# Silu of the gate in the feed-forward and expert steps: ScalarE's own function in place of tanh and a VectorE operation

## The chip, the cores and the metric

The kernel runs on one core of one Trainium2 chip. The metric is the device time of one execution in microseconds (us), as the median of several runs. Beside it stands one profiled execution, from which all durations below are read. TensorE (PE) does the matrix products, VectorE (DVE) and GpSimd (POOL) the elementwise work, ScalarE (ACT) the functions, and SyncE issues the transfers.

## What is computed

Four sequences of 512 positions and width 512 pass through two decoder layers, each of three residual blocks with a layer norm behind each. What matters here are the state scans and the two gated steps:

```python
def _L0_ffn_ref(x, w_gate, w_up, w_down):            # 512 -> 2048 -> 512
    gated = jax.nn.silu(gate) * up
...
def _swiglu(x, wg, wu, wd):                          # 8 experts of 352 and a shared one of 1408
    return jax.nn.silu(x @ wg) * (x @ wu) @ wd
...
def step(state, inp):                                # scan over time, 16 states per channel
    d, b, c, u = inp
    dA = jnp.exp(d[..., None] * A)
    state = state * dA + (d * u)[..., None] * b[:, None, :]
    y = jnp.einsum('bdn,bn->bd', state, c)
```

All eight experts are computed for each position, and their hidden values are multiplied by the routing weight. silu(x) is x times the logistic function of x, which is also x (1 + tanh(x/2)) / 2.

## The kernel before

Everything is held with the channel on the 128 partitions and the 512 positions of one sequence along the free dimension. The four sequences are computed one after the other, three in a loop and the last behind it. The dense products run in bfloat16 in three parts (high by high, high by low, low by high: `product`, L262 to L266), so one 128 by 128 block of weights costs three matmuls of 512 columns.

The gated steps are in `hidden_and_scan`. It runs once per sequence as "ffn" (16 tiles of 128 hidden channels) beside the state scan of the following block (16 blocks of 32 channels), and once as "moe" (33 tiles: 22 of the experts, 11 of the shared one) beside the first scan of the next sequence (32 blocks). The last sequence's "moe" has no scan beside it. Before the first sequence it runs once with a scan and no tiles. So there are 4 feed-forward stages of 16 tiles and 4 expert stages of 33, 196 tiles in all.

In each stage a loop over steps is written out for each engine, and this writing alone sets the order. In a step:

- **TensorE** spreads the scan's u dt and dt over the states for the blocks to come (`spread_dtx`, L673, and `spread_dt`, L661: fp32 matmuls on 32 rows), then `gate` and `up` of the next tile (12 matmuls each), every fourth step `reduce_quad` (L682, the sum over states), then one `down_piece` (up to 12 matmuls), whose bank is free again when VectorE has taken the piece before it (`taken`). `spread_dt(s)` waits until `decays(s - 1)` has read the one bank of dt.
- **ScalarE** does `decays` (L754: four exps of 128 by 511 from PSUM, into one of two buffers `da`, so it waits for the scan of two blocks earlier) and then `gate_tanh` (L761), which reads the gate bank and writes tanh(x/2) into one of two buffers `t2`. Both are in program order: the tanh of tile j stands between the exps of blocks j and j + 1. It waits for the gate product and, from tile 2 on, for `hid` of two tiles earlier.
- **VectorE** does `scan` (L794), `inputs` of the next block (L785), `take_down` (L831, L834), every fourth step `finish_y` (L799), then `silu_gate` (L804), `times_up` (L812), in the expert stages `times_weight` (L820, one to three pieces by partition), `low_part` (L248) and, in the expert stages every fourth step, `inputs_of` (L789). In the expert stages TensorE's `spread_dtx` needs the result of `inputs_of`.
- **GpSimd** multiplies each scanned block by the output rows (L869); `reduce_quad` waits for four of these.

silu thus takes three operations: tanh(x/2) on ScalarE, (t + 1) x on VectorE, and times_up with the factor 0.5. `silu`, the semaphore that VectorE raises, also tells TensorE that a gate bank is free (`gate` of tile j waits for tile j - 2).

```python
    def gate_tanh(jt):
        act.wait_ge(gate_mm, jt + 1)
        if jt >= 2:
            act.wait_ge(hid, jt - 1)
        act.activation(t2[jt % 2], gate_bank(jt), ACT.Tanh, scale=0.5).then_inc(th, 1)
...
    def silu_gate(jt):
        dve.wait_ge(th, jt + 1)
        dve.scalar_tensor_tensor(out=t2[jt % 2], in0=t2[jt % 2], scalar=1.0, in1=gate_bank(jt),
                                 op0=ALU.add, op1=ALU.mult).then_inc(silu, 1)
```

ScalarE's functions lie in sets of tables. The compiler puts an ACT_TABLE_LOAD before an operation whose function isn't in the set that is active. exp and tanh share a set, so the gated stages had no load inside.

Of the kernel before, what the change touches and what calls it, by code (L numbers as in the profile page):

```python
# [8 lines left out]
ALU = mybir.AluOpType  # L9
ACT = mybir.ActivationFunctionType  # L10
# [39 lines left out]
def chunk_of(tiles, j):  # L50

    return (j - first_chunk(tiles)) // CHUNK + 1
# [193 lines left out]
def low(engine, out, x):  # L246

    return engine.tensor_tensor(out, x, high(x), ALU.subtract)  # L248
# [338 lines left out]
def hidden_and_scan(nc, k, tag, tiles, slot, which, gated, last, splitter=None):  # L587
# [14 lines left out]
    with ExitStack() as ctx:  # L602
        def sem(name):
            return k.sem(f"{tag}_{name}")
# [3 lines left out]
        def split_now(step, lag=0):  # L608

            if not splitter or step >= blocks:  # L610
                return []
            count = len(splitter.slots)
            first, end = [at * (count + 2) // blocks for at in (step, step + 1)]
            return [n - lag for n in range(first, end) if 0 <= n - lag < count]
        gate_mm, up_mm, th, silu, hid, weighted = [sem(n) for n in ("gate_mm", "up_mm", "th", "silu", "hid", "weighted")]
        hidlo, xsplit, down, taken = [sem(n) for n in ("hidlo", "xsplit", "down", "taken")]
        dt_mm, dtx_mm, decay = [sem(n) for n in ("dt_mm", "dtx_mm", "decay")]
        dtx_in = sem("dtx_in")
# [2 lines left out]
        t2 = k.moe_t if gated else k.ffn_t  # L621
        xlo = k.moe_xlo if gated else k.ffn_xlo
        held, held_lo = k.held, k.held_lo
        HELD = 2 * CHUNK
# [5 lines left out]
        def down_bank(p):  # L630
            return k.ps[:, 3 + p % KM if last_chunk(p) else 7, :]

        def gate_bank(jt):
            return k.ps[:, 3 + jt % 2, :]

        def up_bank(jt):
            return k.ps[:, 5 + jt % 2, :]

        def states(s):
            return k.states[s % NB]  # L640

        def quartet(s):
            return states(s).rearrange("p (n t) -> p n t", n=GRP)

        def weight_pieces(jt):
            return expert_pieces(jt) if jt < ROUTED else [(0, P, NEXP)]

        @blk.sync
        def _(sp):
            stream_block(k, sp, slot + (hidden_slots(tiles) if tiles else 0), last)  # L650
            if splitter:
                splitter.move(sp)
# [94 lines left out]
        @blk.scalar  # L747
        def _(act):
            def decays(s):
                act.wait_ge(dt_mm, s + 1)  # L750
                if s >= 2:
                    act.wait_ge(scanned, s - 1)
                for n in range(GRP):
                    a = act.activation(k.da[s % 2][:, n, 1:T], dt_bank[:, 1:T], ACT.Exp, scale=rate[:, GRP * s + n:GRP * s + n + 1])  # L754
                a.then_inc(decay, 1)

            def gate_tanh(jt):
                act.wait_ge(gate_mm, jt + 1)
                if jt >= 2:
                    act.wait_ge(hid, jt - 1)  # L760
                act.activation(t2[jt % 2], gate_bank(jt), ACT.Tanh, scale=0.5).then_inc(th, 1)  # L761

            if blocks:
                decays(0)
            if tiles:
                gate_tanh(0)
            for step in range(steps):
                if step + 1 < blocks:
                    decays(step + 1)
                if step + 1 < tiles:  # L770
                    gate_tanh(step + 1)
                for n, late in zip_longest(split_now(step), split_now(step, 2)):
                    if late is not None and splitter.by_pe(late):
                        splitter.take_rest(act, late)
                    if n is not None:
                        splitter.high_part(act, n)

        @blk.vector
        def _(dve):

            def inputs(s):
                dve.wait_ge(dtx_mm, s + 1)
                if s >= NB:
                    dve.wait_ge(reduced, (s - NB) // 4 + 1)
                dve.tensor_tensor(quartet(s), dtx_bank[:, None, :].broadcast_to([P, GRP, T]), k.in_rows, ALU.mult).then_inc(inp, 1)  # L785

            def inputs_of(j):

                dve.tensor_tensor(k.dtx_now[:, j % 2, :], dt[:, j, :], y[:, j, :], ALU.mult).then_inc(dtx_in, 1)  # L789

            def scan(s):
                dve.wait_ge(decay, s + 1)
                dve.wait_ge(inp, s + 1)
                dve.tensor_tensor_scan(states(s), k.da[s % 2][:, :, :].rearrange("p n t -> p (n t)"), states(s), 0.0,  # L794
                                       ALU.mult, ALU.add).then_inc(scanned, 1)

            def finish_y(j):
                dve.wait_ge(reduced, j + 1)
                dve.scalar_tensor_tensor(out=y[:, j, :], in0=y[:, j, :], scalar=skip[:, j:j + 1], in1=y_bank,  # L799
                                         op0=ALU.mult, op1=ALU.add).then_inc(yout, 1)  # L800

            def silu_gate(jt):
                dve.wait_ge(th, jt + 1)
                dve.scalar_tensor_tensor(out=t2[jt % 2], in0=t2[jt % 2], scalar=1.0, in1=gate_bank(jt),  # L804
                                         op0=ALU.add, op1=ALU.mult).then_inc(silu, 1)

            def times_up(jt):
                dve.wait_ge(silu, jt + 1)
                dve.wait_ge(up_mm, jt + 1)
                if jt >= HELD:  # L810
                    dve.wait_ge(down, KM * chunk_of(tiles, jt - HELD) + KM)
                dve.scalar_tensor_tensor(out=held[:, jt % HELD, :], in0=t2[jt % 2], scalar=0.5, in1=up_bank(jt),  # L812
                                         op0=ALU.mult, op1=ALU.mult).then_inc(hid, 1)

            def times_weight(jt):

                h = held[:, jt % HELD, :]
                dve.wait_ge(hid, jt + 1)
                for a, b, e in weight_pieces(jt):
                    op = dve.tensor_tensor(h[a:b, :], h[a:b, :], k.gates[a:b, e, :], ALU.mult)  # L820
                op.then_inc(weighted, 1)

            def low_part(jt):
                dve.wait_ge(weighted if gated else hid, jt + 1)
                low(dve, held_lo[jt % HELD], held[:, jt % HELD, :]).then_inc(hidlo, 1)

            def take_down(p):
                m = p % KM
                dve.wait_ge(down, p + 1)
                if p < KM:  # L830
                    dve.tensor_copy(k.xc[:, m, :], down_bank(p)).then_inc(taken, 1)  # L831
                else:
                    dve.wait_ge(taken, p + 1 - KM)
                    dve.tensor_tensor(k.xc[:, m, :], k.xc[:, m, :], down_bank(p), ALU.add).then_inc(taken, 1)  # L834

            if which == 0:
                inputs_of(0)
            if tiles:
                for c in range(KM):
                    low(dve, xlo[:, c, :], k.xr[:, c, :]).then_inc(xsplit, 1)  # L840
            if blocks:
                inputs(0)
            for step in range(steps):
                if step < blocks:
                    scan(step)
                    for n in split_now(step, 1):
                        if not splitter.by_pe(n):
                            splitter.low_part(dve, n)
                if step + 1 < blocks:
                    inputs(step + 1)  # L850
                if LAG <= step < pieces + LAG:
                    take_down(step - LAG)
                if step % 4 == 1 and 5 <= step <= blocks + 1:
                    finish_y(step // 4 - 1)
                if step < tiles:
                    silu_gate(step)
                    times_up(step)
                if gated and step < tiles:
                    times_weight(step)
                if step < tiles:  # L860
                    low_part(step)
                if which == 0 and step % 4 == 2 and step + 2 < blocks:
                    inputs_of(step // 4 + 1)
# [1035 lines left out]
```

## Time and profile before

| | us |
|---|---|
| median of 3 runs | 4571.92 (4571.24 to 4577.19) |
| profiled execution, its own time | 4570.23 |
| its span, first to last instruction | 4568.5 |
| TensorE busy (matmul) | 3618.0, 79% |
| VectorE busy | 3404.5, 75% |
| ScalarE busy | 1331.6, 29% |
| GpSimd busy | 1275.6, 28% |
| mean granted TensorE clock | 0.87 |

The profile's page shows two engines near three quarters busy. It doesn't say which of them ends a wait in a given stage, so the stages are read one by one from the timelines, whose rows give the start, the duration, the engine, the line and what released the engine after an idle time. A matmul's duration there is longer than its spacing, since matmuls overlap. The stages repeat: the sixteen tanh operations of the four feed-forward stages span 145.69, 145.67, 145.70 and 145.69 us from first to last, the thirty-three of the three expert stages with a scan 334.51, 334.48 and 334.48.

### The profile page before, as it was taken

To read this page: it belongs to the slowest core of one execution; us is meant where nothing else is said; L and a number is where in the kernel's file an instruction comes from. 1 tells how busy PE (TensorE), PEld (TensorE's weight loads), DVE (VectorE), ACT (ScalarE), POOL (GpSimd) and SP (SyncE) were. 2 spreads that over 40 slices of the span, in tenths; PEclk is the share of its full clock that TensorE was granted. 3 is DMA by queue.
4 is the path that set the end of the run, shared out by engine and by line. 5 is a ranking of instruction groups with operands and counts; after the bars stand their busy time and mean duration, and the time that the engine had idled before them with its cause. 6 is when DMAs were issued, how large, how long until landed. Compare 5 with 4: busy or idle time off the path is not lost. (4 is left out here: it accounts for less than half of the span.)

```text
span 4568.5 us, 40958 instructions
## 1 busy us (share of the span) xinstructions
PE 3618.0 (79%) x15151; PEld 1519.7 (33%) x15151; DVE 3404.5 (75%) x3068; ACT 1331.6 (29%) x2010; POOL 1275.6 (28%) x440
## 2 busy tenths in 40 slices
PE   5777769846999769857899778965899976984798
PEld 2222333313333333313433333322433323331443
DVE  5989479575899569785799757876699847967444
ACT  4666332114322233113322233211422233211201
POOL 1544114321344104331244202332144311432000
PEclk8888879867999879878799988977799987986899
DMA  4888212201222202111122211110122121220122
GB/s 150 307 325 305 102 35 76 69 14 44 70 76 76 90 27 76 63 35 53 54 76 70 95 42 62 63 56 30 49 76 70 67 97 34 78 69 15 62 97 79
DMA packets 69035, 380.85 MB, mean 83 GB/s; under 512 B 7648, under 2 KB 7776, under 8 KB 66784
## 3 DMA queue, kind: packets, MB, share of 16 engines
q1 hardware_dynamic: 68832, 378.15, 23.7%
q8 instruction: 127, 2.08, 0.2%
q14 instruction: 76, 0.62, 0.0%
HBM read 314.16 MB, written 63.96 MB: 83 GB/s over the span
## 5 line engine op out<-in xcount | busy, mean ns | idle before, releaser
L265 PE MATMUL ps<-r,ring 128*128 128x512 bf16 (+1 forms) x1912 | 751.9, 394 | 0.0
L262 PE MATMUL ps<-xr,ring 128*128 128x512 bf16 x1696 | 681.3, 402 | 33.2 <-DVE r L248 19.9
L266 PE MATMUL ps<-xr,ring 128*128 128x512 bf16 x1696 | 678.7, 400 | 0.0
L869 POOL TENSOR_TENSOR hh<-hh,bc 128x2048 f32<-128x2048 f32 x72 | 336.3, 4671 | 1020.7 <-DVE hh L794 1020.7
L262 PE MATMUL ps<-r,ring 128*128 128x512 bf16 (+4 forms) x1160 | 464.6, 401 | 102.8 <-DVE xc L834 38.3
L754 ACT ACTIVATE da<-ps,params_sb 128x511 f32<-128x511 f32 x768 | 463.1, 691 | 83.5 <-PE ps L661 57.6
L266 PE MATMUL ps<-r,ring 128*128 128x512 bf16 (+4 forms) x1160 | 464.5, 401 | 0.0
L869 POOL TENSOR_TENSOR bc<-bc 128x2048 f32<-128x2048 f32 x64 | 301.1, 4705 | 390.2 <-DVE bc L794 390.2
L869 POOL TENSOR_TENSOR r<-r,bc 128x2048 f32<-128x2048 f32 x56 | 261.9, 4677 | 322.7 <-DVE r L794 322.7
L794 DVE TENSOR_TENSOR_SCAN hh<-da,hh 128x2048 f32<-128x2048 f32 x72 | 326.0, 4527 | 1.5
L794 DVE TENSOR_TENSOR_SCAN bc<-da,bc 128x2048 f32<-128x2048 f32 x64 | 291.6, 4556 | 0.5
L262 PEld LDWEIGHTS ps<-xr,ring 128*128 128x128 bf16 x1696 | 168.0, 99 | 371.9 <-issue 187.3
L661 PE MATMUL ps<-r,squares_sb 32*128 32x512 f32 x384 | 234.0, 691 | 58.5 <-PEq L1710 31.4
L761 ACT ACTIVATE row<-ps 128x512 f32<-128x512 f32 x100 | 59.7, 597 | 744.4 <-PE ps L266 744.4
L262 PE MATMUL ps<-bc,ring 128*128 128x512 bf16 (+3 forms) x416 | 175.0, 421 | 123.3 <-DMA ring<-wsplit 39.2
L834 DVE TENSOR_TENSOR xc<-xc,ps 128x512 f32<-128x512 f32 x176 | 119.6, 680 | 199.3 <-PE ps L266 199.3
L265 PEld LDWEIGHTS ps<-r,ring 128*128 128x128 bf16 (+1 forms) x1912 | 189.0, 99 | 236.4 <-issue 30.9
L794 DVE TENSOR_TENSOR_SCAN r<-da,r 128x2048 f32<-128x2048 f32 x56 | 254.4, 4542 | 0.6
L266 PEld LDWEIGHTS ps<-xr,ring 128*128 128x128 bf16 x1696 | 166.8, 98 | 235.0 <-issue 28.8
L761 ACT ACTIVATE r<-ps 128x512 f32<-128x512 f32 x96 | 57.3, 597 | 603.8 <-PE ps L266 603.8
L262 PEld LDWEIGHTS ps<-r,ring 128*128 128x128 bf16 (+4 forms) x1160 | 113.1, 98 | 330.2 <-issue 174.5
L201 PE MATMUL ps<-r,squares_sb 128*128 128x512 f32 x282 | 175.5, 709 | 52.3 <-ACT ring L226 20.3
(232 smaller groups left out, 6655.0 us busy)
## 6 DMA issues: line engine op xcount, KB each, us to landing
ring<-wsplit SPq DMA_DIRECT2D x304, 768.0 KB, 4.2
r<-wstream SPq DMA_DIRECT2D x76, 768.0 KB, 7.5
wsplit<-ring SPq DMA_DIRECT2D x58, 768.0 KB, 4.8
wsplit<-r SPq DMA_DIRECT2D x18, 768.0 KB, 5.9
bc<-xT SPq DMA_DIRECT2D x4, 1024.0 KB, 5.6
xr<-xT SPq DMA_DIRECT2D x4, 1024.0 KB, 9.4
bc<-guwT SPq DMA_DIRECT2D x4, 1024.0 KB, 11.2
out<-xr SPq DMA_DIRECT2D x4, 1024.0 KB, 3.9
```

The source lines that it names most:

```text
L201: pe.matmul(self.banks[:, c, :], ident, self.whole[n % SPLIT_RING][:, at], start=True, stop=False)
L262: mm = pe.matmul(out, w_hi, x_hi, start=start, stop=False)
L265: pe.matmul(out, w_hi, x_lo, start=False, stop=False)
L266: return pe.matmul(out, w_lo, x_hi, start=False, stop=stop)
L661: pe.matmul(dt_bank, k.headmean[at, :], dt[at, s // 4, :], start=True, stop=True).then_inc(dt_mm, 1)
L754: a = act.activation(k.da[s % 2][:, n, 1:T], dt_bank[:, 1:T], ACT.Exp, scale=rate[:, GRP * s + n:GRP * s + n + 1])
L761: act.activation(t2[jt % 2], gate_bank(jt), ACT.Tanh, scale=0.5).then_inc(th, 1)
L794: dve.tensor_tensor_scan(states(s), k.da[s % 2][:, :, :].rearrange("p n t -> p (n t)"), states(s), 0.0, ALU.mult, ALU.add).then_inc(scanne ...
L834: dve.tensor_tensor(k.xc[:, m, :], k.xc[:, m, :], down_bank(p), ALU.add).then_inc(taken, 1)
L869: pool.tensor_tensor(quartet(s), quartet(s), k.out_rows, ALU.mult).then_inc(read, 1)
```

## The change

ScalarE computes silu directly from the gate bank. `silu_gate` goes away, `times_up` becomes a plain product, and `silu` is raised by ScalarE.

```diff
--- before.py
+++ after.py
@@ -612,7 +612,7 @@
             count = len(splitter.slots)
             first, end = [at * (count + 2) // blocks for at in (step, step + 1)]
             return [n - lag for n in range(first, end) if 0 <= n - lag < count]
-        gate_mm, up_mm, th, silu, hid, weighted = [sem(n) for n in ("gate_mm", "up_mm", "th", "silu", "hid", "weighted")]
+        gate_mm, up_mm, silu, hid, weighted = [sem(n) for n in ("gate_mm", "up_mm", "silu", "hid", "weighted")]
         hidlo, xsplit, down, taken = [sem(n) for n in ("hidlo", "xsplit", "down", "taken")]
         dt_mm, dtx_mm, decay = [sem(n) for n in ("dt_mm", "dtx_mm", "decay")]
         dtx_in = sem("dtx_in")
@@ -754,21 +754,21 @@
                     a = act.activation(k.da[s % 2][:, n, 1:T], dt_bank[:, 1:T], ACT.Exp, scale=rate[:, GRP * s + n:GRP * s + n + 1])
                 a.then_inc(decay, 1)
 
-            def gate_tanh(jt):
+            def gate_silu(jt):
                 act.wait_ge(gate_mm, jt + 1)
                 if jt >= 2:
                     act.wait_ge(hid, jt - 1)
-                act.activation(t2[jt % 2], gate_bank(jt), ACT.Tanh, scale=0.5).then_inc(th, 1)
+                act.activation(t2[jt % 2], gate_bank(jt), ACT.Silu).then_inc(silu, 1)
 
             if blocks:
                 decays(0)
             if tiles:
-                gate_tanh(0)
+                gate_silu(0)
             for step in range(steps):
                 if step + 1 < blocks:
                     decays(step + 1)
                 if step + 1 < tiles:
-                    gate_tanh(step + 1)
+                    gate_silu(step + 1)
                 for n, late in zip_longest(split_now(step), split_now(step, 2)):
                     if late is not None and splitter.by_pe(late):
                         splitter.take_rest(act, late)
@@ -799,18 +799,12 @@
                 dve.scalar_tensor_tensor(out=y[:, j, :], in0=y[:, j, :], scalar=skip[:, j:j + 1], in1=y_bank,
                                          op0=ALU.mult, op1=ALU.add).then_inc(yout, 1)
 
-            def silu_gate(jt):
-                dve.wait_ge(th, jt + 1)
-                dve.scalar_tensor_tensor(out=t2[jt % 2], in0=t2[jt % 2], scalar=1.0, in1=gate_bank(jt),
-                                         op0=ALU.add, op1=ALU.mult).then_inc(silu, 1)
-
             def times_up(jt):
                 dve.wait_ge(silu, jt + 1)
                 dve.wait_ge(up_mm, jt + 1)
                 if jt >= HELD:
                     dve.wait_ge(down, KM * chunk_of(tiles, jt - HELD) + KM)
-                dve.scalar_tensor_tensor(out=held[:, jt % HELD, :], in0=t2[jt % 2], scalar=0.5, in1=up_bank(jt),
-                                         op0=ALU.mult, op1=ALU.mult).then_inc(hid, 1)
+                dve.tensor_tensor(held[:, jt % HELD, :], t2[jt % 2], up_bank(jt), ALU.mult).then_inc(hid, 1)
 
             def times_weight(jt):
 
@@ -853,7 +847,6 @@
                 if step % 4 == 1 and 5 <= step <= blocks + 1:
                     finish_y(step // 4 - 1)
                 if step < tiles:
-                    silu_gate(step)
                     times_up(step)
                 if gated and step < tiles:
                     times_weight(step)
```

The lines of the new kernel behind L799 stand 7 lower than those of the old (`times_up` is L807).

On ScalarE, in the feed-forward stage from tile 2 on, the order before was this (two steps; `da` are the exps of `decays`, `row` and `r` the two buffers `t2`; a wait is shown by the first name that its semaphore had in the program, so `first_landed2` and `first_stored2` are `hid` and `gate_mm` here, `prep0_gdone` and `prep0_weights_in` are `scanned` and `dt_mm`):

```order
L754 ACTIVATE da<-ps,params_sb 128x511 [waits prep0_gdone,prep0_weights_in]
L754 ACTIVATE da<-ps,params_sb 128x511 x3
L761 ACTIVATE row<-ps 128x512 [waits first_landed2,first_stored2]
L754 ACTIVATE da<-ps,params_sb 128x511 [waits prep0_gdone,prep0_weights_in]
L754 ACTIVATE da<-ps,params_sb 128x511 x3
L761 ACTIVATE r<-ps 128x512 [waits first_landed2,first_stored2]
```

Now there are two table loads in each step. Of the two waits the load carries the one for the buffer (`prep0_gsplit` is `scanned`, `first_landed3` is `hid`), the function behind it the one for its input (`prep0_spread` is `dt_mm`, `first_stored2` is `gate_mm`):

```order
L754 ACT_TABLE_LOAD [waits prep0_gsplit]
L754 ACTIVATE da<-ps,params_sb 128x511 [waits prep0_spread]
L754 ACTIVATE da<-ps,params_sb 128x511 x3
L761 ACT_TABLE_LOAD [waits first_landed3]
L761 ACTIVATE row<-ps 128x512 [waits first_stored2]
L754 ACT_TABLE_LOAD [waits prep0_gsplit]
L754 ACTIVATE da<-ps,params_sb 128x511 [waits prep0_spread]
L754 ACTIVATE da<-ps,params_sb 128x511 x3
L761 ACT_TABLE_LOAD [waits first_landed3]
L761 ACTIVATE r<-ps 128x512 [waits first_stored2]
```

So a load can run before its function's input is there. Counted over the whole program this gives 126 loads more as written (31 in a feed-forward stage, 63 in an expert stage with a scan, 1 in the last one), and with the loop 4 x 31 + 3 x 63 + 1 = 314 in an execution.

On VectorE, one step of the feed-forward stage before (L794 is the scan; this listing names it by its operand form):

```order
L794 SCALAR_TENSOR_TENSOR bc<-da,bc 128x2048
L785 TENSOR_TENSOR bc<-ps,bc 128x2048
L804 SCALAR_TENSOR_TENSOR row<-row,ps 128x512
L812 SCALAR_TENSOR_TENSOR r<-row,ps 128x512
L248 TENSOR_TENSOR ctxTs<-r 128x512
L794 SCALAR_TENSOR_TENSOR bc<-da,bc 128x2048
```

and now:

```order
L794 SCALAR_TENSOR_TENSOR bc<-da,bc 128x2048
L785 TENSOR_TENSOR bc<-ps,bc 128x2048
L807 TENSOR_TENSOR r<-row,ps 128x512
L248 TENSOR_TENSOR ctxTs<-r 128x512
L794 SCALAR_TENSOR_TENSOR bc<-da,bc 128x2048
```

One operation of 128 by 512 leaves each step, and the product by `up` is a TENSOR_TENSOR. Nothing else moves on any engine.

## Rows read from the trace of the kernel before

**Rows 1.** Windows: from:to, us; busy PE, PEld, DVE, ACT, POOL; clock, DMA share, GB/s

```profile
638.00:822.00 184.00, 176.38 (x768) 66.23 (x768) 159.90 (x104) 46.91 (x80) 73.31 (x16) 0.94 0.23 78
1147.00:1520.00 373.00, 348.83 (x1594) 134.04 (x1594) 352.73 (x268) 96.58 (x165) 146.98 (x32) 0.98 0.22 72
4270.00:4545.00 275.00, 270.63 (x1239) 120.48 (x1238) 119.48 (x178) 25.07 (x42) 0.00 (x0) 0.99 0.28 95
```

**Rows 2.** Groups of instructions, VectorE: busy us, mean ns, idle before and its releaser

```profile
L834 DVE TENSOR_TENSOR xc<-xc,ps 128x512 f32<-128x512 f32 x176 | 119.6, 680 | 199.3 <-PE ps L266 199.3
...
L804 DVE SCALAR_TENSOR_TENSOR row<-row,ps 128x512 f32<-128x512 f32 x100 | 67.8, 678 | 5.2 <-ACT row L761 5.2
```

**Rows 3.** Timeline of ScalarE: start, us taken, engine, line; a table load between two operations

```profile
627.89 1.23 ACT L927 ACTIVATE xr<-xc 128x512 f32<-128x512 f32 x2 [1.45 <-DVE xc L947]
629.14 1.28 ACT L930 ACT_TABLE_LOAD   x1
630.43 0.20 ACT L930 ACTIVATE warm<-eps 128x1 f32<-128x1 f32 x1
```

**Rows 4.** Timeline of ScalarE, first feed-forward stage

```profile
660.61 0.60 ACT L761 ACTIVATE r<-ps 128x512 f32<-128x512 f32 x1 [7.24 <-PE ps L266]
661.10 2.41 ACT L754 ACTIVATE da<-ps,params_sb 128x511 f32<-128x511 f32 x4
667.49 0.60 ACT L761 ACTIVATE row<-ps 128x512 f32<-128x512 f32 x1 [3.98 <-PE ps L266]
...
689.02 0.60 ACT L761 ACTIVATE r<-ps 128x512 f32<-128x512 f32 x1 [3.99 <-PE ps L266]
...
743.45 0.60 ACT L761 ACTIVATE row<-ps 128x512 f32<-128x512 f32 x1 [9.93 <-PE ps L266]
...
761.77 0.60 ACT L761 ACTIVATE row<-ps 128x512 f32<-128x512 f32 x1 [6.25 <-PE ps L266]
...
783.76 0.60 ACT L761 ACTIVATE row<-ps 128x512 f32<-128x512 f32 x1 [9.93 <-PE ps L266]
```

**Rows 5.** Timeline of TensorE, the same stage: spreads of dt

```profile
663.56 0.69 PE L661 MATMUL ps<-r,squares_sb 32*128 32x512 f32 x1
...
767.00 0.69 PE L661 MATMUL ps<-r,squares_sb 32*128 32x512 f32 x1
```

**Rows 6.** Windows of the first feed-forward stage (columns as in Rows 1)

```profile
653.60:660.40 6.80, 6.80 (x14) 1.94 (x14) 6.73 (x5) 0.00 (x0) 0.13 (x1) 0.50 0.35 116
662.00:689.00 27.00, 26.14 (x107) 10.62 (x106) 24.47 (x15) 10.33 (x18) 12.23 (x3) 1.00 0.31 100
```

**Rows 7.** Timeline of VectorE, the same stage, near its end

```profile
780.98 2.29 DVE L785 TENSOR_TENSOR bc<-ps,bc 128x2048 f32<-128x2048 f32 x1 [1.67 <-PE ps L673]
...
785.88 0.69 DVE L248 TENSOR_TENSOR held_more<-r 128x512 bf16<-128x512 f32 x1
```

**Rows 8.** Timeline of GpSimd, the same stage

```profile
779.39 4.57 POOL L869 TENSOR_TENSOR hh<-hh,bc 128x2048 f32<-128x2048 f32 x1 [4.96 <-DVE hh L794]
```

**Rows 9.** Timeline of VectorE, first expert stage

```profile
1176.36 0.69 DVE L820 TENSOR_TENSOR r<-r 128x512 f32<-128x512 f32 x1
...
1231.92 4.42 DVE L794 TENSOR_TENSOR_SCAN hh<-da,hh 128x2048 f32<-128x2048 f32 x1
...
1240.46 1.08 DVE L820 TENSOR_TENSOR r<-r 128x512 f32<-128x512 f32 x1
...
1242.19 4.42 DVE L794 TENSOR_TENSOR_SCAN bc<-da,bc 128x2048 f32<-128x2048 f32 x1
...
1263.08 0.69 DVE L820 TENSOR_TENSOR r<-r 128x512 f32<-128x512 f32 x1
...
1275.28 4.42 DVE L794 TENSOR_TENSOR_SCAN r<-da,r 128x2048 f32<-128x2048 f32 x1
```

**Rows 10.** Timeline of GpSimd, the same stage

```profile
1236.41 4.58 POOL L869 TENSOR_TENSOR hh<-hh,bc 128x2048 f32<-128x2048 f32 x1 [6.29 <-DVE hh L794]
...
1258.37 4.59 POOL L869 TENSOR_TENSOR bc<-bc 128x2048 f32<-128x2048 f32 x1 [7.08 <-DVE bc L794]
```

## The prediction

> **What bounds the kernel now.** I read four views: windows for whole stages, groups for durations, the timelines of single engines for what each step waits for, and windows again for the clock.
>
> By the windows [rows 1] no single engine fills a gated stage. In the feed-forward stage TensorE is busy 176 of 184 us and VectorE 160. In the expert stage with a scan it is 349 and 353 of 373, so the two are level. In the last expert stage, without a scan, TensorE is busy 271 of 275. ScalarE is busy a quarter of the time at most. So 0.68 us of VectorE work in each of 196 tiles [rows 2], 133 us in all, is only worth what each stage's own chain makes of it.
>
> The feed-forward timeline [rows 4] has two regimes. From 660.61 to 689.02, before any down piece, four steps take 28.41 us, the first of them 6.88. Here the chain is ScalarE to TensorE and back: the exps start 0.49 after the tanh, take 2.41, and the spread of dt that needs their bank starts at once (661.10 + 2.41 = 663.51; 663.56 in [rows 5]). After it comes the next gate product and the next tanh, 3.98 after the exps' end. Later TensorE alone sets the pace: 743.45 to 761.77 is two steps of 9.16, and to 783.76 two more, one of them with a reduction (12.83). There the exps end at 761.77 + 0.49 + 2.41 = 764.67, and TensorE asks for their bank only at 767.00 [rows 5]: 2.33 us of slack. Between the regimes, from 689.02 to 743.45, five steps take 54.43 where TensorE's own work is 3 x 9.16 + 2 x 12.83 = 53.14. The other 1.29 is waiting for VectorE.
>
> The expert stage with a scan is VectorE's. A scan starts at 1231.92 and the next at 1242.19 [rows 9], 10.27 for a plain step. But VectorE doesn't work through that step freely. GpSimd's product runs from 1236.41 to 1240.99 [rows 10], and the operation at L820, which reads two operands from the SBUF, starts at 1240.46 and takes 1.08 where 0.69 is normal: it ends 0.55 after GpSimd's. The plain step is scan, GpSimd's product, 0.55, and the rest. The operations before L820 lie under GpSimd's product.
>
> **The change, part by part.**
>
> *The tables.* ScalarE gets 314 loads. The row of one [rows 3] shows what it costs between two operations: the one before ends at 629.12, the load starts at 629.14, the next at 630.43, so 1.31 us with nothing behind it. Since back-to-back operations otherwise start 0.11 before the end of the one ahead (0.49 against 0.60 in [rows 4]), a load adds 1.42. I take this value; from below the cost is 0 where the load hides, from above twice it (the first rival). The silu load waits only for a buffer, so it runs in the 3.98 us or more in which ScalarE sat idle before each tanh, and costs nothing. If that idle time went below 1.3 us it would show. The exp load always comes between silu and the exps. Where the exps had slack (2.33 us late in the feed-forward stage) it leaves 0.91 and costs nothing. In the early chain it costs all of 1.42.
>
> *Feed-forward, early.* Four steps of 6.88 + 1.42 = 8.30 make 33.20 in place of 28.41: **+4.79** (in the fourth, a wait for VectorE is part of the 28.41 and is covered). The step from the first tanh to the second isn't touched: the exps there wait for TensorE anyway.
>
> *Feed-forward, middle and end.* TensorE now comes late, VectorE is no longer waited for, and the 1.29 goes: TensorE is **3.50** late (4.79 - 1.29) from then on. VectorE waits for it near the end (780.98, idle 1.67, [rows 7]), so the last two steps start 3.50 late. In the first of these L248 starts at 785.88, behind GpSimd's end at 783.96 [rows 8]: the missing 0.68 counts. In the last one it stands behind GpSimd's product and counts nothing. Sum **+2.82** a stage, 11.3 for four.
>
> *Expert stages with a scan.* In a plain step, 0.68 less before L820 changes only how long L820 waits: worth 0. In the second step L820 isn't held (1176.36, 0.69): worth 0.68, once. In a step with `finish_y` L820 starts at 1263.08, behind GpSimd's end at 1262.96. Without the 0.68 it would start at 1262.40 and end 0.55 after GpSimd, at 1263.51 in place of 1263.77: worth 0.26. There are seven such steps with a scan behind them. Sum 0.68 + 7 x 0.26 = **-2.5** a stage, 7.5 for three. The early steps get longer on ScalarE here too, but VectorE's steps of 10.27 are longer than that chain's 8.30, so I cost it at nothing. The cover is these 2 us a step; without it the price would be the feed-forward one, 4.79 a stage.
>
> *Last expert stage.* TensorE-bound, no exps: 0. *times_up* as a TENSOR_TENSOR: 680 ns against 678 [rows 2], and silu like tanh 0.60: both 0. No row has a silu, so its duration is bounded by 0 and by double, 0.6 more, which would add 4 x 4 x 0.6 = 10.
>
> Sum: +11.3 - 7.5 = +3.8 us. Against the profiled execution's own 4570.2 that is 4574.0; its time lies 1.7 under the median of the runs shown, so in terms of the median 4571.9 + 3.8 = 4575.7. I say **4576**. 0.2%, 9 us, is about what a measurement of this kernel can tell from no change, so this is "the same", a little on the slow side.
>
> **The rivals.**
>
> *A load costs twice what the row shows* (slower). The mechanism would be a second idle stretch of the same length beside each load between silu and exp, 2.7 in place of 1.42. The point from which it decides is the 2.33 us of slack: beyond it every late feed-forward step pays too. Early: 4 x 9.6 = 38.4, +10.0. Six plain late steps pay 0.4 each, +2.4. With the -1.29 and -0.68 of above +10.4 a stage, 42 for four; the expert stages give 6 or 7 back. That is +35, 4607. For: nothing in the trace; the load in [rows 3] stands back to back on both sides, if beside other functions. Chance 0.1. The Trainium skill speaks for it: "ScalarE: Activation LUTs", in "What ACT_TABLE_LOAD costs", puts a switch at 1283 ns for the load plus about 1380 ns for a drain, 2.66 us together, and tells the author to do all of one set before switching; by that figure the sum would be this rival's. The load's own 1.28 agrees with this case's rows; the drain isn't in them.
>
> *The clock falls in the early steps* (slower). TensorE would idle 1.4 us more in each of them. It had 1.0 from 662 to 689 and 0.50 just before [rows 6]. If it fell for one such stretch of 6.8 us in each of seven stages, some 3.4 us of work each, that gives up to +14 on the feed-forward stages and little on the others: 4590. For: in the stage's first steps it was at that half, the lower of its two levels. Against: TensorE was busy 26.1 of those 27 us [rows 6], and with 1.42 of idle time in 8.30 it is still busy 80% of them. Chance 0.12.
>
> *VectorE's time counts in full* (faster). If the hold by GpSimd moved with the work, each expert step would be 0.68 shorter. Three steps and a plain fourth, 1231.92 to 1275.28, take 43.36; less 2.7 is 40.6, just over TensorE's 3 x 9.16 + 12.83 = 40.3. That is -2.7 x 8 x 3 = -65, with the feed-forward stages' +11 some -54: 4518. Against: every L820 that meets GpSimd ends 0.55 after it. Chance 0.06.
>
> *The loads are hidden everywhere*, also in the early chain: only the gains stay, 4564 to 4568. Chance 0.05.
>
> **How the numbers follow.** My forecast has 0.67, and its own range is 4567 to 4586: half of the feed-forward cost, or silu longer by 0.6. The range of 8 in 10 takes in the clock rival: 4564 to 4594, leaving out the double load and VectorE's full gain. Same: the forecast nearly whole, part of the hidden-load case and a third of the clock's, 0.70. Slower: 0.22. Faster: 0.08.
>
> **What would show it.** Right: 314 loads of 1.28 on ScalarE; silu at 8.3 us spacing four times in each feed-forward stage, then 9.16 and 12.83 with no idle time of TensorE; 149 us from its first to its last silu in place of 145.7; 332 in the expert stages in place of 334.5; L820 in plain expert steps longer, near 1.8, and ending 0.55 after GpSimd's. Wrong: a gap beside the loads; windows at half clock among the early steps; plain expert steps under 10.2.

## The result, and the profile after

| | us |
|---|---|
| before, median of 6 runs | 4572.1 (4569.4 to 4577.2) |
| changed, median of 6 runs | 4592.6 (4588.2 to 4596.5) |
| ratio | 1.0044, 95% interval 1.0031 to 1.0056 |
| changed, profiled execution: its own time, its span | 4588.2, 4586.4 |

The kernel is slower by 0.44%, more than the 0.2% that can be told from no change. I had said 4576, "the same", with a range of 4564 to 4594. The time lies inside the range, but outside the forecast's own 4567 to 4586, and the most likely case was the wrong one. When measured again (e5, below) the changed kernel was slower by 0.21%.

What the groups of ScalarE and VectorE show (busy us, mean ns, idle before):

```profile
L761 ACT ACT_TABLE_LOAD x161 | 206.6, 1283 | 3.9 <-DVE r L807 0.9 <-PEq L1463 0.3
L754 ACT ACT_TABLE_LOAD x154 | 197.6, 1283 | 20.2 <-PEq L290 6.6 <-DVE bc L794 4.6 <-DVE hh L794 3.0
...
L761 ACT ACTIVATE row<-ps 128x512 f32<-128x512 f32 x100 | 59.7, 597 | 548.8 <-PE ps L266 548.8
```

```profile
L807 DVE TENSOR_TENSOR r<-row,ps 128x512 f32<-128x512 f32 x100 | 67.9, 679 | 7.3 <-PE ps L266 7.3
```

There are 161 + 154 = 315 loads in the two places, where one had been before: 314 more, of 1283 ns each. silu takes 597 ns, as tanh did, and the product 679. So the counts and prices were right.

The windows of the first feed-forward stage, the first expert stage, and then three short stretches of the feed-forward one (columns as in [rows 1]):

```profile
645.00:830.00 185.00, 174.91 (x734) 65.32 (x749) 152.78 (x86) 88.00 (x111) 73.05 (x16) 0.93 0.22 73
1158.00:1530.00 372.00, 348.48 (x1570) 135.46 (x1600) 350.22 (x235) 181.07 (x230) 146.85 (x32) 0.99 0.22 72
681.70:685.10 3.40, 3.40 (x9) 1.09 (x9) 3.37 (x4) 0.39 (x1) 2.73 (x1) 0.50 0.36 108
685.10:691.90 6.80, 6.05 (x22) 2.19 (x22) 6.03 (x2) 5.49 (x7) 2.51 (x1) 1.00 0.16 64
691.90:695.30 3.40, 3.40 (x9) 1.17 (x9) 3.37 (x4) 0.09 (x1) 2.01 (x1) 0.50 0.53 168
```

ScalarE went from 47 to 88 us busy in a feed-forward stage, VectorE from 160 to 153. The last three rows are the finding: TensorE's granted clock is 0.50 for 3.4 us, 1.00 for 6.8 us, 0.50 again. Before, the four steps that correspond to these ran at 1.00 [rows 6]. 1.00 is 2.4 GHz, 0.50 is 1.2 GHz.

The timeline of ScalarE in the same stage, which answers to [rows 4]:

```profile
668.15 0.60 ACT L761 ACTIVATE r<-ps 128x512 f32<-128x512 f32 x1 [5.92 <-PE ps L266]
668.77 1.28 ACT L754 ACT_TABLE_LOAD   x1
670.06 2.42 ACT L754 ACTIVATE da<-ps,params_sb 128x511 f32<-128x511 f32 x4
672.50 1.28 ACT L761 ACT_TABLE_LOAD   x1
676.46 0.60 ACT L761 ACTIVATE row<-ps 128x512 f32<-128x512 f32 x1 [2.68 <-PE ps L266]
...
686.36 0.60 ACT L761 ACTIVATE r<-ps 128x512 f32<-128x512 f32 x1 [4.28 <-PE ps L266]
...
696.31 0.60 ACT L761 ACTIVATE row<-ps 128x512 f32<-128x512 f32 x1 [4.32 <-PE ps L266]
...
706.25 0.60 ACT L761 ACTIVATE r<-ps 128x512 f32<-128x512 f32 x1 [4.31 <-PE ps L266]
...
719.09 0.60 ACT L761 ACTIVATE row<-ps 128x512 f32<-128x512 f32 x1 [7.21 <-PE ps L266]
...
759.41 0.60 ACT L761 ACTIVATE row<-ps 128x512 f32<-128x512 f32 x1 [7.21 <-PE ps L266]
...
799.73 0.60 ACT L761 ACTIVATE row<-ps 128x512 f32<-128x512 f32 x1 [7.21 <-PE ps L266]
...
808.88 0.60 ACT L761 ACTIVATE r<-ps 128x512 f32<-128x512 f32 x1 [3.53 <-PE ps L266]
```

- The silu load (672.50) runs in the wait for the gate product, the exp load (668.77) stands between silu and exps: 668.15 to 676.46 is 8.31 us, where 6.88 had been. That is the 1.42 of the forecast.
- The next three spacings are 9.90, 9.95 and 9.94, and not 8.3.
- From 706.25 on every step is TensorE's: 12.84, and 9.16 for a step without a reduction. 759.41 to 799.73 is 40.32, as the four steps in [rows 4] were 40.31. VectorE isn't waited for.
- First to last silu is 808.88 - 654.80 = 154.1 us against 145.7, in all four stages. I had 149.

TensorE just before the first of the slow gate products:

```profile
679.02 1.12 PE L673 MATMUL ps<-r,squares_sb 32*128 32x512 f32 x2
680.84 1.28 PE L661 MATMUL ps<-r,squares_sb 32*128 32x512 f32 x2 [0.70 <-ACT da L754]
682.05 0.61 PE L262 MATMUL ps<-xr,ring 128*128 128x512 bf16 x1
```

The last product ends, the spread of u dt runs (679.02), then TensorE waits 0.70 us for the exps, spreads dt, and the clock is already down. The first matmul of the gate product (682.05) takes 0.61 us where 0.39 is normal. Before, the two spreads ran side by side, 0.4 us apart, with no wait: the one of dt is the first row of [rows 5], the one of u dt beside it is

```profile
663.16 0.69 PE L673 MATMUL ps<-r,squares_sb 32*128 32x512 f32 x1
```

The step just ahead of this one had the same wait (0.69 us) and kept the clock. Its window, columns as before:

```profile
670.73:679.02 8.29, 7.43 (x28) 2.81 (x28) 7.10 (x4) 5.56 (x9) 1.21 (x1) 1.00 0.27 95
```

TensorE was busy 7.43 of 8.29 us in it, 90%.

The expert stage on VectorE and GpSimd, answering to [rows 9, 10]:

```profile
1242.09 4.42 DVE L794 TENSOR_TENSOR_SCAN hh<-da,hh 128x2048 f32<-128x2048 f32 x1
...
1249.92 1.81 DVE L814 TENSOR_TENSOR r<-r 128x512 f32<-128x512 f32 x1
...
1252.37 4.42 DVE L794 TENSOR_TENSOR_SCAN bc<-da,bc 128x2048 f32<-128x2048 f32 x1
...
1272.54 1.16 DVE L814 TENSOR_TENSOR r<-r 128x512 f32<-128x512 f32 x1
```

```profile
1246.59 4.59 POOL L862 TENSOR_TENSOR hh<-hh,bc 128x2048 f32<-128x2048 f32 x1 [6.29 <-DVE hh L794]
...
1268.55 4.59 POOL L862 TENSOR_TENSOR bc<-bc 128x2048 f32<-128x2048 f32 x1 [7.08 <-DVE bc L794]
```

L814 is L820 of the kernel before, L862 its L869. In the plain step it now takes 1.81 us, ends at 1251.73, 0.55 after GpSimd (1251.18), and the step is 1252.37 - 1242.09 = 10.28. The missing operation has only lengthened the wait. In the step with `finish_y` L814 waits as well (1.16 where 0.69 had been), which is worth the 0.26 that was forecast. First to last silu of the three stages is 332.3, 332.3 and 332.2 us against 334.5. The last scan of the stage comes 2.51 us earlier after the first silu than it did after the first tanh, by 0.72 in the second step and by about a quarter of a microsecond in each of the seven steps with `finish_y`.

In this pair of profiles 7.6 of the 17.9 us of span lie ahead of the first silu (654.80 against 647.23). That part is the same code. In the eight profiles further on the first tanh or silu starts anywhere from 645.2 to 650.4, whatever the kernel, and with the changed kernel itself at 645.2 (e5). So the 7.6 don't come again with the change. From the first tanh or silu to the first of the last expert stage it is 3638.9 us before and 3649.5 now, 10.6 longer. That is the stretch with the changed code.

### The profile page after: what moved, and what is told of

It reads as the page before. It is cut to its first block and busy times, and to the rows that moved or that the text cites. A ratio compares the mean times of both kernels' runs of the same rounds, so it can differ in the third digit from the quotient of the medians.

```text
span 4586.4 us, 40808 instructions
## 1 busy us (share of the span) xinstructions
PE 3603.8 (79%) x14892; PEld 1521.6 (33%) x15151; DVE 3352.8 (73%) x2872; ACT 1746.5 (38%) x2324; POOL 1270.4 (28%) x440
## 5 line engine op out<-in xcount | busy, mean ns | idle before, releaser
L265 PE MATMUL ps<-r,ring 128*128 128x512 bf16 (+1 forms) x1862 | 736.7, 396 | 13.6 <-DVE r L248 8.2
L262 PE MATMUL ps<-xr,ring 128*128 128x512 bf16 x1653 | 667.8, 404 | 30.0 <-DVE r L540 14.5
L266 PE MATMUL ps<-xr,ring 128*128 128x512 bf16 x1655 | 666.7, 403 | 2.5
L862 POOL TENSOR_TENSOR hh<-hh,bc 128x2048 f32<-128x2048 f32 x72 | 336.1, 4669 | 1046.9 <-DVE hh L794 1046.9
L262 PE MATMUL ps<-r,ring 128*128 128x512 bf16 (+3 forms) x1129 | 447.9, 397 | 71.9 <-DVE xc L828 31.6
L266 PE MATMUL ps<-r,ring 128*128 128x512 bf16 (+4 forms) x1145 | 456.0, 399 | 1.3
L862 POOL TENSOR_TENSOR bc<-bc 128x2048 f32<-128x2048 f32 x64 | 297.5, 4649 | 393.1 <-DVE bc L794 393.1
L862 POOL TENSOR_TENSOR r<-r,bc 128x2048 f32<-128x2048 f32 x56 | 261.3, 4666 | 326.1 <-DVE r L794 326.1
L794 DVE TENSOR_TENSOR_SCAN hh<-da,hh 128x2048 f32<-128x2048 f32 x72 | 325.1, 4515 | 1.5
L265 PE MATMUL ps<-bc,ring 128*128 128x512 bf16 (+2 forms) x463 | 192.3, 415 | 148.8 <-POOL bc L248 64.1
L794 DVE TENSOR_TENSOR_SCAN bc<-da,bc 128x2048 f32<-128x2048 f32 x64 | 290.4, 4538 | 0.5
L794 DVE TENSOR_TENSOR_SCAN r<-da,r 128x2048 f32<-128x2048 f32 x56 | 255.0, 4554 | 0.6
L920 ACT ACTIVATE xr<-xc 128x512 f32<-128x512 f32 x96 | 58.9, 630 | 417.6 <-DVE xc L940 417.6
```

Source lines behind the costliest of these rows:

```text
L262: mm = pe.matmul(out, w_hi, x_hi, start=start, stop=False)
L265: pe.matmul(out, w_hi, x_lo, start=False, stop=False)
L266: return pe.matmul(out, w_lo, x_hi, start=False, stop=stop)
L862: pool.tensor_tensor(quartet(s), quartet(s), k.out_rows, ALU.mult).then_inc(read, 1)
L920: act.activation(half(k.xr, h, pair), half(k.xc, h, pair), ACT.Square).then_inc(sq, 1)
```

## The experiments

Two theories. **A**: TensorE falls to the lower clock in the early feed-forward steps, since each now has a wait in it; this was the second rival of the prediction. **B**: the extra time comes from the loads as such, wherever they are, or from the longer program. "Span" below is the time from the first to the last of a stage's tanh or silu operations, from the timelines; "distance" that from a stage's first to the next stage's first.

### One kind of stage at a time

```diff
+        native = not gated            # e1: feed-forward stages;  e2: native = gated, expert stages
...
+                if native:
+                    act.activation(t2[jt % 2], gate_bank(jt), ACT.Silu).then_inc(silu, 1)
+                    return
                 act.activation(t2[jt % 2], gate_bank(jt), ACT.Tanh, scale=0.5).then_inc(th, 1)
...
+                if native:
+                    dve.tensor_tensor(held[:, jt % HELD, :], t2[jt % 2], up_bank(jt), ALU.mult).then_inc(hid, 1)
+                    return
...
-                    silu_gate(step)
+                    if not native:
+                        silu_gate(step)
```

> Only the four feed-forward stages use ScalarE's silu; the expert stages keep tanh and the VectorE operation. Theory A (the early feed-forward steps fall to the lower TensorE clock once each waits 1.42 us for the exp load): first to last silu 154.1 us in these stages as in the changed kernel, against 145.7; the expert stages as before, 334.5; together about +21 us, 4593. Theory B (the extra time comes from the loads wherever they are, or from the longer program, outside these steps): the feed-forward stages give the +11 us that the rows before gave, and the rest of the +20 stays away or shows ahead of the first gated stage.

> Only the expert stages use ScalarE's silu. Theory A: 332.3 us from first to last silu in place of 334.5, feed-forward stages as before at 145.7; together -7 to -10 us, 4562 to 4565, faster than both kernels. Theory B: 189 of the 314 loads are here, so more than half of the +20 us stays, 4580 or more.

### The VectorE operation alone, the loads alone

```diff
 # e3, on the changed kernel (leaves the gate's function out: tanh in its place)
-                act.activation(t2[jt % 2], gate_bank(jt), ACT.Silu).then_inc(silu, 1)
+                act.activation(t2[jt % 2], gate_bank(jt), ACT.Tanh, scale=0.5).then_inc(silu, 1)
 # e4, on the kernel before
             def gate_tanh(jt):
+                act.activation(k.touch[:, jt:jt + 1], k.eps, ACT.Silu)
                 act.wait_ge(gate_mm, jt + 1)
```

> The changed kernel with tanh(x) in the place of silu(x), so no table load in a gated stage and one VectorE operation less; the gate's function is left out of the output. It prices the VectorE operation alone. If most of it lies under GpSimd's product, as the rows before say: about -2 us in a feed-forward stage (the 1.29 of waiting and 0.68 at its end), -2.5 to -3 in an expert stage with a scan, together -15 us, 4557; a plain expert step stays 10.27 from scan to scan. If VectorE's time counted in full: 0.68 a step, 4510 to 4520.

> The kernel before, plus a one-element silu ahead of each tanh (nothing else of the computation changes): the same table loads in the same places as in the changed kernel, the VectorE operation kept. Theory A: feed-forward stages near 154 us from first to last tanh with the same stretches at half clock, expert stages within 1 us of 334.5; together +22 to +30 us, 4594 to 4602. Theory B: the expert stages grow too, by 5 us or more each.

The four ran on one chip, beside 17 runs of the kernel before (median 4574.9):

| | median us | ratio, 95% interval | span, feed-forward | span, expert |
|---|---|---|---|---|
| before | 4574.9 | | 145.7 | 334.5 |
| e1, silu in the feed-forward stages | 4593.8 | 1.0037 (1.0024 to 1.0050) | 154.1 | 334.5 |
| e2, silu in the expert stages | 4568.8 | 0.9985 (0.9976 to 0.9994) | 145.7 | 332.2 |
| e3, the operation gone, no loads | 4555.1 | 0.9957 (0.9944 to 0.9970) | 144.7 | 332.2 |
| e4, loads alone | 4609.9 | 1.0076 (1.0064 to 1.0088) | 154.1 | 334.5 |

All of the loss is in the feed-forward stages: +19 us with 124 of the added loads (64 + 61 in e1's groups, less the one of before), while the other 190, in the expert stages, go with a gain of 6 (I had expected 7 to 10). B falls. The loads in the expert stages cost nothing at all: e4's span there is the 334.5 of the kernel before. In the feed-forward stages e4 has the 154.1 of the changed kernel with the VectorE operation in place:

```profile
666.02 1.28 ACT L758 ACT_TABLE_LOAD   x1
667.31 0.20 ACT L758 ACTIVATE touch<-eps 128x1 f32<-128x1 f32 x1
669.99 0.60 ACT L762 ACTIVATE row<-ps 128x512 f32<-128x512 f32 x1 [2.47 <-PE ps L266]
670.60 1.28 ACT L754 ACT_TABLE_LOAD   x1
...
679.90 0.60 ACT L762 ACTIVATE r<-ps 128x512 f32<-128x512 f32 x1 [4.07 <-PE ps L266]
```

The load and the small silu (666.02, 667.31) are out of the way before the tanh, the exp load (670.60) isn't, and the next tanh comes after 9.91 us. e4 cost 35 us, more than the 22 to 30 that I expected. Its distances from a feed-forward stage to the next expert stage are 515.2 us against 508.4 or 505.1 before, so 6.8 or 10.2 more. With the last stage's 10.2 that is 34.0 us, so nearly all of the 35 lies in the feed-forward stages and what follows them, where the spans alone grew by 4 x 8.4 = 33.6.

e3 prices the operation: -20 us of the 133 that VectorE saves. I had expected -15. The plain expert step stays as it was, held by GpSimd:

```profile
1229.97 4.42 DVE L794 TENSOR_TENSOR_SCAN hh<-da,hh 128x2048 f32<-128x2048 f32 x1
...
1237.80 1.80 DVE L814 TENSOR_TENSOR r<-r 128x512 f32<-128x512 f32 x1
...
1240.24 4.42 DVE L794 TENSOR_TENSOR_SCAN bc<-da,bc 128x2048 f32<-128x2048 f32 x1
```

```profile
1234.47 4.58 POOL L862 TENSOR_TENSOR hh<-hh,bc 128x2048 f32<-128x2048 f32 x1 [6.29 <-DVE hh L794]
```

1237.80 + 1.80 = 1239.60 is 0.55 after GpSimd's end at 1239.05, and 1229.97 to 1240.24 is 10.27.

### Is it the clock? Matmuls for nobody

```diff
                 if step + 1 < blocks:
                     spread_dtx(step + 1)
+                if not gated and tiles and 1 <= step <= 4:
+                    for _ in range(4):
+                        pe.matmul(k.ps[:, 7, :], k.identb, xlo[:, 0, :], start=True, stop=True)
                 if step + 2 < blocks:
                     spread_dt(step + 2)
```

> The changed kernel with four more matmuls of 512 columns, into a bank that nobody reads, between the two spreads of feed-forward steps 1 to 4, where TensorE waits 0.7 us for the exps. Theory A (the clock falls because TensorE has too little to do there): the steps between silu 2 and silu 5 return from 9.9 to about 8.3 to 8.5 us, the clock reads 1.0 in them, first to last silu 149 to 150 in place of 154.1, and the time falls by 3.4 to 5 us a stage, 14 to 20 in all. Rival: the 9.9 us comes from the load or the bank itself, then the steps get longer by the filler (0.1 to 0.4 us each) and nothing falls.

Beside it ran the changed kernel itself:

> The changed kernel once more, to see it beside its variants on one chip. The two halves of the change gave +19 and -6 in medians when run alone, so if they add up it is 12 to 15 us over the kernel before, and near 20 if the first measurement stands. The time up to the first silu (654.8 us in the first profile, 647 to 650 in five others) tells whether the part ahead of the gated stages has a share in the difference: 648 to 651 if it was chance, 655 again if the change does it.

The chip was another one than that of e1 to e4 (before: median 4576.1 of 27 runs). The changed kernel took 4585.8 (ratio 1.0021, 1.0012 to 1.0030), 9.8 us over the kernel before, less than the 12 to 15 that the halves had led me to expect. With the filler it was 4570.7 (0.9991, 0.9982 to 1.0000). So sixteen matmuls more in each feed-forward stage make it 15 us faster. TensorE with the filler (L734), between the two spreads:

```profile
672.67 1.12 PE L673 MATMUL ps<-r,squares_sb 32*128 32x512 f32 x2
673.72 1.04 PE L734 MATMUL ps<-r,identb 128*128 128x512 bf16 x4
674.69 1.12 PE L661 MATMUL ps<-r,squares_sb 32*128 32x512 f32 x2
675.75 0.40 PE L262 MATMUL ps<-xr,ring 128*128 128x512 bf16 x1
```

and the window over its early steps, columns as before:

```profile
661.30:695.50 34.20, 33.80 (x127) 12.51 (x129) 29.48 (x15) 22.33 (x28) 16.31 (x4) 1.00 0.23 78
```

The clock is 1.00 in the whole of it. The spacing of silus is 8.51 four times (8.31 and 0.20 for matmuls beyond the 0.70 of waiting), and the span is 150.0 in place of 154.1. A stands. The table loads are as many as in the changed kernel, so they aren't what made these steps 9.9 us long. The run doesn't tell what it takes to hold the clock, only that it held with four matmuls more in the gap.

### Taking the exps off the chain

```diff
+            ahead = 1 if tiles else 0
             if blocks:
                 decays(0)
             if tiles:
                 gate_silu(0)
+            if blocks and ahead:
+                decays(1)
             for step in range(steps):
-                if step + 1 < blocks:
-                    decays(step + 1)
+                if step + 1 + ahead < blocks:
+                    decays(step + 1 + ahead)
                 if step + 1 < tiles:
                     gate_silu(step + 1)
```

> The changed kernel, but in the gated stages ScalarE does the exps of block s + 2 ahead of the silu of tile s + 1, so the exps no longer stand behind a gate product and a load. If the cost of the change is the chain TensorE, silu, load, exps, TensorE of the early feed-forward steps, it goes: these steps are TensorE's own 6.3 to 6.5 us, first to last silu at most 145 us, the gains on VectorE stay, and the whole lies near the 4555 of the variant without loads, 4550 to 4560, faster than the kernel before. If the loads cost by their number (there are as many, less a few), it stays at 4585 or more.

> The same order of the exps in the kernel before (tanh and the VectorE operation kept). The early feed-forward steps go from 6.89 to 6.3 to 6.5 us, but VectorE's step of 9.55 follows, so first to last tanh falls by 0 to 2 us a stage; expert stages as before: 4565 to 4575. The difference between this and the run above is then the worth of ScalarE's silu when its loads are off the chain: -10 to -15 us.

On the second chip e7 took 4557.2 us (ratio 0.9956, 0.9942 to 0.9969) and e8 4576.9 (0.9997, 0.9988 to 1.0006). e7 is faster than both kernels, with 300 loads more than before. ScalarE in e7's first feed-forward stage:

```profile
667.80 1.28 ACT L761 ACT_TABLE_LOAD   x1
669.10 0.60 ACT L761 ACTIVATE row<-ps 128x512 f32<-128x512 f32 x1
673.35 1.28 ACT L754 ACT_TABLE_LOAD   x1 [3.66 <-DVE bc L797]
674.65 2.42 ACT L754 ACTIVATE da<-ps,params_sb 128x511 f32<-128x511 f32 x4
677.08 1.28 ACT L761 ACT_TABLE_LOAD   x1
678.37 0.60 ACT L761 ACTIVATE r<-ps 128x512 f32<-128x512 f32 x1
```

The exps (674.65) now wait for VectorE's scan and not for a gate product, and the silu behind them (678.37) finds its product ready. Both loads stand in the row of ScalarE's work that the scan sets off, but ScalarE still sits idle 3.66 us ahead of it, and from 668.86 to 704 VectorE goes from one operation to the next without a wait, so the loads hold nobody up. From the third step on the steps are VectorE's, 9.3 to 9.6 us (10.0 and 10.6 for two late ones with a `finish_y` and a wait for TensorE), the clock is full, the span 145.0. I had said TensorE's 6.3 to 6.5 for these steps, which is a miss: the exps run two blocks ahead into two buffers, so they follow the scans from the third step on. The total was as expected. With tanh the new order is worth nothing: e8's early steps take 6.50 and 8.27 us and then VectorE's 9.5, and the span is the 145.7 of before, since the old chain of 6.89 us was shorter than VectorE's step already. The difference of e7 and e8 is 20 us, where I had expected 10 to 15, and it is what e3 gave for the VectorE operation.

## Why the prediction was right or wrong

- *What bounds the kernel*: right. All loads that I had called hidden are hidden (expert span in e4 unchanged).
- *The tables*, 1.42 on the chain, silu load free: right (8.31 forecast 8.30). *A load costs twice*, the first rival: did not happen. The Trainium skill's figure, 2.66 us for a switch ("ScalarE: Activation LUTs", "What ACT_TABLE_LOAD costs"), isn't what these rows show: 668.75 to 670.06 is 1.31 us from the end of silu to the exps.
- *Feed-forward, early*, +4.79 a stage: **this is the step that failed.** It priced all four steps at 8.30. One was; three were at 9.9, since the clock fell in them. 3 x 1.6 = 4.9 us a stage were missing, which is the 154.1 against 149 of the span. The second rival had the mechanism, at 3.4 us a stage and a chance of 0.12. Its price was a third too low. The chance rested on a busy share of 80%. The share was in fact 90% in the step ahead of the first fall, since the two spreads, with the wait between them, no longer overlap and take longer, and the clock fell all the same. So the share was no ground. The time still lies in the range, since the range took this rival in. Some 2.2 us of that busy time are fp32 spreads on 32 of 128 rows; whether this matters to the clock isn't tested.
- *Feed-forward, middle*: -1.29, right; no step waits for VectorE, 706.25 to 759.41 is 53.16 against the 53.14 forecast.
- *Expert stages*: -2.5 a stage, measured -2.2 from first to last silu and -2.5 to the last scan. The 0, 0.26 and 0.55 of the single operations were all found. *VectorE's time counts in full*: did not happen.
- *The sum*: my terms gave +3.8; 4 x 4.9 = 20 more gives +23, near the first measurement (+20.5) and well over the second (+9.8). That nearness is in part luck. At the end of a feed-forward stage the sum is right: +2.82 and 4.9 are 7.7, and the last scan comes 156.47 us after the first silu where it came 148.81 after the first tanh. But the next stage doesn't start 7.7 later. The distance to it is 511.9 us against 508.4 or 505.1, so only 3.5 or 6.8 more. I had counted nothing behind the stage.

The windows there (kernel before, then changed) differ in the clock:

```profile
800.00:812.00 12.00, 10.83 (x52) 3.29 (x53) 6.21 (x6) 0.00 (x0) 4.51 (x1) 0.72 0.20 67
816.00:828.00 12.00, 10.31 (x62) 3.83 (x64) 6.61 (x6) 0.00 (x0) 4.29 (x1) 1.00 0.20 67
```

Whether this is what gives time back is not tested. From the first tanh or silu to the first of the last expert stage, the two profiles of the changed kernel are 10.6 and 13.9 us longer than that of the kernel before. e1 is 20.5 longer there and e2 6.8 shorter, together 13.7, so the halves add up. Their ratios, multiplied, give 1.0022. Why the first measurement showed 1.0044 and the second 1.0021, with intervals that just don't meet, stays open; in the first profile 7.6 us of it lie ahead of the gated stages.

## What to carry to other kernels

A small wait put into a chain that TensorE is part of can cost twice: the wait, and then the lower clock behind it. TensorE's busy share doesn't tell whether that will happen: here it was 90% in the step before the clock fell. And where an engine does two kinds of work in turn, the one that others wait for should not stand behind the one that waits. Moving the exps turned a loss of 10 to 20 us into a gain of 19, and with that order the table loads cost nothing that shows (e7's ratio is 0.9956, that of e3 without loads 0.9957).

## What the runs showed of the hardware

- The clock fell to 1.2 GHz in steps whose longest wait of TensorE was 0.70 us, between fp32 spreads on 32 rows; and it held at 2.4 GHz with four matmuls of 128 by 512 in the gap (e6).
- A table load took 1283 ns in all 315 places of the gated stages. Of these, 116 stand between silu and exps with no wait on either side, and there the exps started 1.31 us after the end of the silu.
- The tables loaded for silu also served tanh: in e4 no load stands between the small silu and the tanh behind it (667.31 to 669.99).
- Stage distances moved in steps, not smoothly. For the three expert stages with a scan, the distance to them from the feed-forward stage ahead was about 505.0, 508.4, 512.0 or 515.2 us in all ten profiles, and the one from them to the next feed-forward stage about 556.5 or 559.9. So a span shorter by 2.3 us gave 3.4 in the distance (e2), and one shorter by 1.0 also 3.4, or nothing where the distance had been 505.1 before (e3). The same kernel shows more than one of these values (before: 508.4 and 505.1; changed: 511.9 and, in e5, once 515.2), so a single distance can't price a small change. The starts of stages, whose first products run at half clock until it rises, may be what puts them into step. That reading is not tested.
